# A metaformer layer on one core: the bias of the first normalization as one VectorE operation instead of two on GpSimd

## The reference, cut to what matters

```
u   = (x - mean(x, -1)) / sqrt(var(x, -1) + 1e-6)
q, k, v = 1x1 convolutions of u;  attn = softmax(q k^T / sqrt(H W)) per head
o   = 1x1 convolution of (attn v)
x1  = x + layernorm(o, eps 1e-5) * gamma + beta
```

## Time and profile before

| | |
|---|---|
| runs of the kernel | 2418.85, 2418.95 and 2420.6 us, median 2418.95 |
| the profiled execution | 2421.3 us |
| its span, from first to last instruction | 2419.6 us |
| mean granted TensorE clock | 0.901 |
| DMA | 447.75 MB, 185 GB/s |

### The profile page before, as it was taken

One profiled execution on the slowest core, in us unless ns is written; L12 is line 12 of the kernel. 1 busy time (PEld: TensorE's weight loads), 2 busy tenths in 40 slices (PEclk: granted clock), 3 DMA queues, 4 the chain that ended last, 5 costly groups with the idle time before them and its releaser, 6 DMA issues.

```text
span 2419.6 us, 42280 instructions
## 1 busy us (share of the span) xinstructions
PE 2044.8 (85%) x11801; PEld 1470.5 (61%) x11801; DVE 1888.8 (78%) x4793; ACT 1896.7 (78%) x4817; POOL 1988.7 (82%) x2070
## 2 busy tenths in 40 slices
PE   5799999999999999999999999999976556999920
PEld 4666666666666666666666666666632224899920
DVE  3489899999999999999999999999988859311110
ACT  7999999999999999999999999999944331222200
POOL 1199999999999999999999999999999966000087
PEclk9999999999999999999999999999999865555565
DMA  4388888888888888888888888888665541355233
GB/s 153 120 240 219 217 213 232 220 223 213 226 228 221 212 217 228 223 220 218 235 214 222 210 226 225 223 216 233 169 154 140 157 131 43 106 151 155 79 35 34
DMA packets 111054, 447.75 MB, mean 185 GB/s; under 512 B 10573, under 2 KB 52404, under 8 KB 61684
## 3 DMA queue, kind: packets, MB, share of 16 engines
q1 hardware_dynamic: 81140, 302.61, 37.6%
q0 software_dynamic: 29696, 142.61, 32.4%
HBM read 306.78 MB, written 138.41 MB: 184 GB/s over the span
## 4 chain that ended last, share of the span: by engine, by line
POOL 31%; ACT 24%; PE 17%; issue 16%; DVE 10%; DMA 1%; POOLq 0%; SPq 0%; ACTq 0%; DVEq 0%
POOL U L369 11%; ACT U L471 11%; POOL U L374 10%; PE T L663 5%; ACT UT L429 4%; POOL zn L390 3%; ACT zT L435 3%; POOL out_dram L407 3%; PE G L654 2%; PE O L654 2%; ACT LTS L444 2%; PE O L557 2%; PE G L624 2%; ACT LTS L485 2%; POOL U L381 2%
## 5 line engine op out<-in xcount | busy, mean ns | idle before, releaser
L471 ACT ACTIVATE U<-xa,nA,rA 128x128 f32<-128x128 f32 x2048 | 837.2, 481 | 0.6 <-issue 0.6
L369 POOL TENSOR_TENSOR U<-U,bet 128x512 f32<-128x512 f32 x512 | 679.3, 1327 | 0.8
L624 PEld LDWEIGHTS G<-UT 128*128 128x128 f32 x4096 | 536.8, 192 | 228.8 <-issue 224.1
L390 POOL TENSOR_TENSOR zn<-U,rZ 128x512 f32<-128x512 f32 x512 | 585.8, 1144 | 15.2 <-PE T L613 13.2
L374 POOL TENSOR_TENSOR U<-U,rO 128x512 f32<-128x512 f32 x512 | 560.3, 1094 | 9.7 <-ACT rO L453 9.7
L624 PE MATMUL G<-UT 128*128 128x128 f32 x4096 | 542.7, 276 | 0.0
L557 PE MATMUL O<-U,MT 128*128 128x512 f32 x1024 | 528.0, 597 | 0.0
L606 PE MATMUL T<-ident,U 128*128 128x128 f32 x2048 | 323.3, 281 | 128.8 <-ACT UT L429 113.3
L745 DVE BATCH_NORM_STATS2 stA<-xa 128x6 f32<-128x256 f32 x1024 | 385.0, 422 | 59.7 <-DMA xa<-in_x 48.9
L727 DVE BATCH_NORM_STATS2 stO<-O 128x6 f32<-128x256 f32 x1024 | 384.7, 419 | 55.3 <-PE O L557 54.7
L606 PEld LDWEIGHTS T<-ident,U 128*128 128x128 f32 x2048 | 222.6, 142 | 335.3 <-issue 301.3
(11 more groups left out here) (139 smaller groups left out, 2013.2 us busy)
## 6 DMA issues: line engine op xcount, KB each, us to landing
xa<-in_x SPq DMA_DIRECT2D x128, 1024.0 KB, 6.2
U<-in_x POOLq DMA_DIRECT2D x128, 1024.0 KB, 9.0
out_dram<-U SPq DMA_DIRECT2D x128, 1024.0 KB, 7.8
U<-in_L_ffn_weight SPq DMA_DIRECT2D x128, 256.0 KB, 2.9
xa<-out_dram,U POOLq DMA_INDIRECT x64, 2.7
out_dram<-U POOLq DMA_INDIRECT x64, 3.3
U<-in_L_ffn_weight SPq DMA_DIRECT2D x1, 128.0 KB, 2.5
LTS<-in_L_conv_wq SPq DMA_DIRECT2D x1, 64.0 KB
```

What stands on the lines that cost most here:

```text
L369: gp.tensor_tensor(rows(a, i), rows(a, i), bet_b, ALU.add).then_inc(S["gb"], 1)
L390: gp.tensor_tensor(zn[:, i % 2, :].rearrange("p (h w) -> p h w", w=W), rows(a, i), rZ[:, k % 2, i % IC * TI:(i % IC + 1) * TI].unsqueeze(2 ...
L471: last = sc.activation(utile(a, i, j), xa[:, k % XR, h * W:(h + 1) * W], ACT.Identity, scale=rA[:, k % 2, h:h + 1], bias=nA[:, k % 2, h:h ...
L624: last = te.matmul(G[:, 0:P], v, v, start=(i == 0 and j == 0), stop=(i == NI - 1 and j == TI - 1))
```

## The change

The two POOL operations go away, and with them the wait between them. DVE gets one operation that computes (mean * -1) * rA. It stands in DVE's step between L_BNO and L_BNA, with the same two waits that POOL had ahead of it. The semaphore a_nmu now goes up once per chunk instead of twice, and its three waits are counted anew. The hunks below are, in this order, in POOL's body, in ACT's (twice) and in DVE's (twice).

```
-                    if r := item(b, t, L_NMU, IC):
-                        a, k = r
-                        pool.wait_ge(S["a_rstd"], cnt(a, NK, k + 1))
-
-                        wait(pool, S["u_ready"], cnt(a, NI, IC * (k - 1)))
-                        gp.tensor_tensor(nA[:, k % 2, :], stA[:, k % 2, :, 1], rA[:, k % 2, :], ALU.mult).then_inc(S["a_nmu"], 1)
-                        pool.wait_ge(S["a_nmu"], cnt(a, 2 * NK, 2 * k + 1))
-                        gp.tensor_scalar(nA[:, k % 2, :], nA[:, k % 2, :], -1.0, None, ALU.mult).then_inc(S["a_nmu"], 1)
                     if r := item(b, t, L_BETA):
...
-                        wait(act, S["a_nmu"], cnt(a, 2 * NK, 2 * (k - 1)))
+                        wait(act, S["a_nmu"], cnt(a, NK, k - 1))
                         sc.activation(rA[:, k % 2, :], sA[:, :], ACT.Exp, scale=-0.5).then_inc(S["a_rstd"], 1)
...
-                        act.wait_ge(S["a_nmu"], cnt(a, 2 * NK, 2 * k + 2))
+                        act.wait_ge(S["a_nmu"], cnt(a, NK, k + 1))
...
+                    if r := item(b, t, L_NMU, IC):
+                        a, k = r
+                        dve.wait_ge(S["a_rstd"], cnt(a, NK, k + 1))
+
+                        wait(dve, S["u_ready"], cnt(a, NI, IC * (k - 1)))
+                        ve.scalar_tensor_tensor(nA[:, k % 2, :], stA[:, k % 2, :, 1], -1.0, rA[:, k % 2, :],
+                                                ALU.mult, ALU.mult).then_inc(S["a_nmu"], 1)
                     if r := item(b, t, L_BNA):
...
-                            wait(dve, S["a_nmu"], cnt(a, 2 * NK, 2 * (k - 1)))
+                            wait(dve, S["a_nmu"], cnt(a, NK, k - 1))
```

## The result

The changed kernel takes 2526.1 us (median of 4 runs, 2511.8 to 2538.3); the kernel before, run beside it, 2419.8 us. The ratio is 1.043, with a 95% interval of 1.0375 to 1.0491: slower by 106 us. The profiled run took 2523.2 us, with a span of 2521.4. The forecast was 2439 us with a range of 2405 to 2640: right in direction, the time inside the range, and the size missed. The likeliest case alone had reached only to 2472.

The account below looks back on a forecast made before the run. POOL was taken to bound the kernel at 114.3 us per image; DVE would take over at 116.0, +24 us over 14.4 images, less 4 us regained: 2441 us profiled, 2439 us median, range 2405 to 2640.

Parts of the forecast that it names:

- likeliest case: DVE becomes the bound through eight ordinary holds per image: 2439 us, ends 2424 to 2472, chance 0.48.
- The bound before and POOL's relief: POOL sets the pace at 114.3 us per image; without the bias it needs 108.5 and no longer bounds.
- The 9 us of gain: Gain on ACT: 4 us from its idle time, 5.0 us from its waits for transposes behind late zn.
- The waits in front of the new operation: DVE's waits for rA and for the previous chunk's u, ahead of the new operation: cost nothing.
- The price of the operation: New DVE operation, held by POOL, priced at L808's mean: 0.83 us each, 6.6 us per image.
- arithmetic check of 0.69: Random arrival in POOL's cycle: mean rest 0.54 us plus some 0.15 us of work, 0.69 us per operation.
- The waits that were to close: DVE's 2.9 us per image of attention-chain waits would mostly close when DVE comes late, keeping 0.6 us.
- The sum 108.8 + 6.6 + 0.6 = 116.0 us: DVE's busy time, new operations and kept waits per image, +1.7 us against 114.3, over 14.4 images +24 us.
- Rival 2: Starvation: without POOL's self-wait its instructions overlap and DVE finds no gap; 2575 or 2675 us, chance 0.29.
- What I held against it: Against starvation: POOL, needing 108.5 us, must wait now and then, closing the overlap; one DMA's 0.2 us may be too little.
- Its other price: Starvation's costlier variant: four holds per image, each half of 10.5 us, given as 132.1 us per image, 2675 us.
- The signs I had named: New operation's median near 0.8 us, ending behind POOL's ends; several-us holds or L374 above 1.2 us would point to starvation.

Follow-up runs that it names:

- e4_none: Changed kernel without the new DVE operation; the bias stays zero and ACT waits for rA instead: 2416.9 us, 0.9977 of the kernel before.
- e1_reduce: Changed kernel with the new DVE operation replaced by a one-input negating reduce, same place and waits, product with rA left out: 2419.2 us.
- x8_join_ramp: Changed kernel plus two POOL waits for itself after each accumulate DMA, behind the next zn and behind the next beta addition: 2422.4 us.
- e3_dummy: Kernel before, POOL unchanged, with the new DVE operation added and its result unused: 2427.1 us, 1.0022 of the kernel before.
- e2_join: Changed kernel plus one POOL wait for itself per chunk, behind the zn that follows each DMA: 2431.0 us.
- x5_pool_nowait: Kernel before without POOL's self-wait; its second small operation negates rA into a scratch, and DVE gets nothing new: 2489.2 us, 1.0286 of before.
- x9_no_acc: Changed kernel with POOL's 128 accumulate DMAs each replaced by a one-element memset, no self-wait: 2409.9 us.
- x7_split_join: Kernel before with the bias split: DVE negates the mean with one input, POOL makes one product and waits for it: 2414.4 us.
- x10_split_zn: Bias split (DVE negates the mean, POOL makes one product), POOL waiting for itself behind the zn after each DMA: 2409.6 us, 0.9955 of before.
- x11_split_both: Bias split (DVE negates the mean, POOL makes one product), POOL waiting both behind its product and behind the zn after each DMA: 2414.2 us.
- x6_split: Kernel before with the bias split: DVE negates the mean with one input, POOL makes one product, no self-wait: 2420.2 us.

## Why the prediction was right or wrong

**The bound before and POOL's relief: right.** POOL no longer bounds, ACT's floor was put at 114.0 us per image, and e4_none runs at 114.4. The 9 us of gain without a price on DVE were too much: e4_none gained 4.8 us, none of it by the steady pace.

**The waits in front of the new operation cost nothing: right.** The page shows 22.1 us in nine waits for rA, in the filling of the pipeline, and e1_reduce, with the same waits, is no slower than before.

**The price of the operation, 0.83 us as a mean of L808: the step that failed.** It stood for two things at once and was wrong for both. As a plain hold it is too high: the means are 0.488 us in x8_join_ramp and 0.659 in e3_dummy, near the arithmetic check of 0.69 that I had worked out and set aside. At this price the pace is 115.3 us per image in x8_join_ramp and e2_join, +1.0 and not the +1.7 of the forecast, and the whole kernel is 2.7 us over the kernel before beside it in x8_join_ramp (within its noise), 5.4 in e3_dummy and 9.3 in e2_join (with one long hold), not 20. DVE was not even the bound there: in x8_join_ramp it is busy 987.2 of 1028.7 us. As the price in the changed kernel 0.83 us is too low: the mean is 1.352 us, and the cast, which the sum left at its old length, took 3.2 us more per image.

**The waits that were to close: failed too.** Of DVE's 2.9 us per image in the attention chain the sum kept 0.6. In the changed kernel DVE idles 3.7 us per image, and its attention waits are 2.7 us per image from 400 to 1860 us. The sum 108.8 + 6.6 + 0.6 = 116.0 us came out as 108.8 + 10.3 + 3.7 = 122.8, the measured pace but for rounding.

**Rival 2 was the mechanism; I gave it 0.29.** It named the lost self-wait, the overlap and the cause of the overlap. That the self-wait is what matters x5_pool_nowait and e2_join show, each from its side (+70 us without it, -95 us with it). That the overlap is what passes DVE over is shown less well, as three long holds in x9_no_acc came without it. What I held against it failed: "one DMA's overlap, 0.2 us, may be too little". In the changed kernel it was enough: 118 of the 139 ends passed over at such an overlap had only one DMA between them and POOL's last idle time. That POOL must wait now and then was true, and it makes the price milder than the rival's: not one hold of 10.5 us per image (125.1 us) but two to three of 2 to 6 us, cut short when POOL runs dry, and the cast's: 122.9 us. (Its other price, four holds of half of 10.5 us per image, adds up to 133.1 us per image and 2690 us, not 132.1 and 2675.) The signs I had named spoke with two voices: the median of the new operation was 0.69 us and its ends mostly just behind POOL's, as forecast, while y's median stayed at 1.045 us, and only the mean and the maximum (1.161 and 2.211 us) showed what happened.

**The range** held by the bounds from rival 2, not by the likeliest case, whose upper end was 2472. That 2526.1 us lies inside is no merit of the sum behind 2439.

The Trainium skill (SBUF — State Buffer, Who interferes with whom) has the one that comes second blocked until the other instruction finishes. Where POOL's instructions overlap by less than 0.06 us the changed kernel's trace agrees (58 ends of 58 let DVE in); where they overlap by 0.2 us or more it does not (2 of 141), and neither do the three long holds of x9_no_acc. So the rule's price of one instruction, at most 1.3 us here without overlap, is a floor.

## What to carry to other kernels

A semaphore wait that looks like pure cost can be what lets another engine in: before you merge or move operations, ask what waits go away with them, and who used the gap. For a short operation that shares a resource look at the mean, the maximum and the sum beside the median, and at operations nobody touched. If POOL issues DMAs between long rows of operations and DVE does SBUF to SBUF work, try one wait of POOL for its own last result after each DMA: it took 95 us off here (e2_join), and it ended the long holds of the last images too (9.94 and 11.01 us in x7_split_join, 0.49 and 0.56 in x10_split_zn). One is enough: with two of them x11_split_both is 4.6 us slower than x10_split_zn.

## What was not expected of the hardware

- A self-wait of POOL restores its instructions to 1.04 us; so does an idle time of 0.5 us (x6_split). Without either, the overlap grows with each DMA: x5's zn behind six DMAs in a row (1072 to 1142 us) lasts 1.24, 1.30, 1.51, 1.63, 1.83 and 1.96 us, at unchanged distances of 1.00 us between starts.
- Two inputs aren't needed to be held: the cast (one input, 128x8) was held up to 11.02 us, much as the two-input operation (12.26), while the one-input reduce on 128x16 never took more than 0.24 us in 128 (e1_reduce), beside the same POOL. So a small two-input operation can be split: x6_split negates on DVE with one input and leaves the product to POOL.
- A longer record isn't a slower instruction: POOL's two bias operations in x5 have means of 0.69 and 0.72 us, against 0.40 and 0.25 before, but start 0.19 us apart (1157.93 and 1158.12) where it was 0.50.
